# Cross-attention and mixture-of-experts kernel: scores head by head, rounds in three steps, and value products of 33 columns

## The chip, the cores and the metric

The kernel runs on one core of a Trainium2 chip. The metric is the device time of one launch in microseconds (us); lower is better. Times are given as the median of several runs, and one execution was recorded by the hardware profiler.

## What is computed

Inputs are x and ctx, both 8 x 512 x 256 in fp32. For each of the 8 batch rows an mLSTM-like attention with 8 heads of 32 columns runs over 512 positions, with q from x and k = v = ctx; then a feed-forward layer with 2 shared and 8 routed experts (top 2) follows.

```
ifg = concat(q, k, v);  ig = ifg @ igate_w.T + b;  log_f = log_sigmoid(ifg @ fgate_w.T + b)
log_D = cumsum(log_f)[s] - cumsum(log_f)[t] + ig[t]      (t <= s, else -inf)
D = exp(log_D - max(log_D))
C = (q_h @ k_h.T / sqrt(32)) * D                         (per head h)
h = C @ v_h / (max(|sum C|, exp(-max log_D)) + 1e-6)
x = x + layernorm(h) * ln_scale
u = layernorm(x);  x = x + u + shared_experts(u) + top2 routed_experts(u)
```

## The kernel before

The program is two blocks. The second runs the routed experts (39 tiles of 256 sorted tokens) and is not changed. The first, some 760 us of the span, does the attention, the router and the shared experts batch by batch. Only the attention's rounds in it are changed.

**The attention of a batch** is cut into J = 4 chunks of P = 128 positions. Positions of earlier chunks reach a later one through a state matrix (`state`, line 1022), so each chunk j is one round that works on a diagonal block of 128 x 128 positions for all NH = 8 heads. A round has these parts:

- exponents, on TensorE (lines 1037 and 1039): for each half of four heads (g = 0, 1) a bf16 product of the identity with the causal mask (128 rows, 512 columns) starts a bank and a bf16 product of `exp_lhs` with `exp_rhs` (56 rows, 512 columns) adds the exponents. Banks 0 and 1 of the four attention banks.
- decay, on ScalarE (line 567): exp of both banks into `decay`.
- scores, on TensorE (line 1048): for each g one fp32 product of k (`qcT`) with `qmask`, 128 rows and 512 columns, into banks 2 and 3. `qmask` holds q four times, each copy zeroed outside the 32 rows of one head. Half of it is made by VectorE (line 698, four multiplications of 128 x 512), half by GpSimd (line 475, four too).
- ct, on VectorE (line 767): scale, scores and decay multiplied, two operations of 128 x 512.
- value products, on TensorE: the state's part (line 1066, for j > 0, bank 0), and then for each head a product of ct with `vaug` (line 1071). A head's values are 33 columns (32 and a column of ones for the row sum), but each product streams PW = 99 columns, of which 33 are used.
- hn, on VectorE (lines 775, 781 and 783): the results out of PSUM, two operations per round for the values and one more for the state's part.

**The order** of the first block is written out by hand: `START`, `FIRST`, `ORDER` and `ORDER_6` are lists of letters, and every engine walks them and does its own part of each letter. "U" is one unit of the shared experts (16 per batch): up products (line 1119), gelu and a rounding on ScalarE (lines 590 and 593), a subtraction on VectorE (line 835), and, two units later, down products (line 1102). The digits are the steps of the rounds: each digit is written twice, the first for exponents and scores of a round, the second for its value products. They run in pass b for batch b + 1, between the units of batch b. "S" is the state, "L" the last down products of the batch before, "H" the handing over of the tokens to the shared experts (lines 629 and 849), "Y" the finished sum (line 842) and its store. "A", "Q", "B", "D", "E" belong to the router; "F", "G", "M", "R", "C", "c" to the front of the batch after (norm, transposes, gates, cumulative sums); "T", "V", "W", "X" to the norms after the attention. Batch 0's attention stands in `START`, where no units run yet; "w" there is the splitting of one piece of the shared weights (ScalarE line 622 or 624, VectorE line 678 or 681).

```
ORDER = "S 0 L H Y 0 U 1 A U 1 F U Q 2 U F 2 B U P 3 U 3 D U G M T E U T U Z T U Z R V U V U V U R U W U X C U c".split()
```

## Time and profile before

| what | value |
|---|---|
| median of 3 runs | 1243.25 us (1241.1 to 1245.12) |
| the profiled execution | 1241.27 us |
| its span | 1239.5 us |
| TensorE busy | 1137.4 us |
| VectorE busy | 919.4 us |
| ScalarE busy | 837.6 us |
| GpSimd busy | 341.8 us |
| TensorE's mean granted clock | 0.964 |

A profile row names an instruction by its source line, engine, operation and tiles. The timeline gives start (us), duration (us) of a merged group, and in brackets how long the engine had been idle before it and what ended the idle time. Matmuls are pipelined: the durations of neighbours overlap, so the pitch is read from start to start. One fp32 product on TensorE appears as two matmul records (a group "x4" is two products); a transpose and an fp32r or bf16 product appear as one.

### The profile page before, as it was taken

The numbers are of one execution on the slowest core, as the hardware profiler recorded it, in microseconds if no ns is written. First come the engines' busy times: TensorE is split into PE (matmuls) and PEld (weight loads), VectorE is DVE, ScalarE is ACT, GpSimd is POOL, SyncE is SP. The second block draws the span as 40 slices with busy tenths as digits, with TensorE's granted clock in tenths as the row PEclk, the third lists the DMA queues.
The fourth block names the chain that finished last, engine by engine and source line by source line (L and its number), as shares of the span: only waits on it lengthen the run. The fifth ranks groups of instructions, "written<-read, shape, count | busy, mean of one in ns | idle before, by whom it ended". The sixth has DMA issues, their size and how long they took to land. (4 is left out here: it accounts for less than half of the span.)

```text
span 1239.5 us, 21821 instructions
## 1 busy us (share of the span) xinstructions
PE 1137.4 (92%) x7861; PEld 996.7 (80%) x7861; DVE 919.4 (74%) x2215; ACT 837.6 (68%) x1441; POOL 341.8 (28%) x319
## 2 busy tenths in 40 slices
PE   2748999999989999989989897999999999999996
PEld 1436776886777777777868787999999999999996
DVE  5885696686777777866955564888888888888883
ACT  3526556566476556565664353999999999999994
POOL 7121221510510412313113020233333233333333
PEclk9776999999999999999999898999999999999998
DMA  6110011111010100110001035788888888888872
GB/s 197 34 35 17 34 36 35 36 35 35 35 52 23 65 27 32 46 35 35 19 17 44 1 121 170 219 220 233 239 212 232 244 208 232 244 209 230 246 186 27
DMA packets 141692, 136.17 MB, mean 110 GB/s; under 512 B 48599, under 2 KB 127585, under 8 KB 141585
## 3 DMA queue, kind: packets, MB, share of 16 engines
q1 hardware_dynamic: 122948, 111.68, 28.6%
q0 software_dynamic: 14304, 18.75, 9.2%
q10 hardware_dynamic: 4332, 4.34, 1.0%
q8 instruction: 63, 1.03, 0.3%
q14 instruction: 45, 0.36, 0.1%
HBM read 109.42 MB, written 25.33 MB: 109 GB/s over the span
## 5 line engine op out<-in xcount | busy, mean ns | idle before, releaser
L1358 DVE TENSOR_TENSOR wlo<-big,whi 128x512 fp32r<-128x512 f32 x312 | 219.9, 716 | 21.8 <-ACT whi L1311 14.4
L1311 ACT CAST whi<-big 128x512 fp32r<-128x512 f32 x312 | 191.2, 615 | 6.5 <-PEq L420 5.1
L590 ACT ACTIVATE shared_hraw<-bank,b1s 128x512 f32<-128x512 f32 x128 | 88.1, 688 | 153.9 <-PE bank L1119 153.6
L1283 PE MATMUL bank<-xhi,whi 128*128 128x256 f32 x624 | 175.6, 281 | 6.3 <-DVE xlo L1372 5.1
L1261 PE MATMUL bank<-whi,hhi 128*128 128x256 f32 x624 | 178.1, 285 | 0.0
L1283 PE MATMUL bank<-xhi,wlo 128*128 128x256 f32 x624 | 174.5, 280 | 0.0
L1261 PE MATMUL bank<-wlo,hhi 128*128 128x256 f32 x624 | 174.4, 280 | 0.0
L1261 PE MATMUL bank<-whi,hlo 128*128 128x256 f32 x624 | 174.4, 280 | 0.0
L1283 PE MATMUL bank<-xlo,whi 128*128 128x256 f32 x624 | 174.3, 279 | 0.0
L1333 ACT ACTIVATE hraw<-bank,b 128x256 f32<-128x256 f32 x312 | 147.9, 474 | 36.2 <-PE bank L1283 35.3
L835 DVE TENSOR_TENSOR shared_hlo<-shared_hraw,shared_hhi 128x512 fp32r<-128x512 f32 x128 | 93.1, 731 | 96.4 <-ACT shared_hhi L593 92.9
L495 POOL DMA_INDIRECT sorted_tokens<-rowbuf,slots x64 | 66.7, 1042 | 322.5 <-DVEq L911 305.5
L1102 PE MATMUL bank<-whs,shared_hhi 128*128 128x256 f32 x512 | 150.2, 293 | 3.8 <-DVE shared_hlo L835 3.8
L1402 DVE TENSOR_TENSOR hlo<-hraw,hhi 128x512 fp32r<-128x512 f32 x156 | 108.0, 693 | 55.3 <-ACT hhi L1338 49.7
L1102 PE MATMUL bank<-whs,shared_hlo 128*128 128x256 f32 x512 | 146.0, 285 | 0.0
L1102 PE MATMUL bank<-wls,shared_hhi 128*128 128x256 f32 x512 | 145.9, 285 | 0.0
L1436 POOL DMA_INDIRECT out_dram<-yt,token x78 | 135.4, 1736 | 29.3 <-issue 18.7
L1119 PE MATMUL bank<-xhs,whs 128*128 128x512 f32 x256 | 118.1, 461 | 9.5 <-ACT shared_hraw L590 5.9
L1283 PEld LDWEIGHTS bank<-xhi,whi 128*128 128x128 f32 x624 | 118.9, 190 | 6.7 <-POOL xhi L1425 5.3
L1283 PEld LDWEIGHTS bank<-xlo,whi 128*128 128x128 f32 x624 | 119.0, 191 | 0.0
L1283 PEld LDWEIGHTS bank<-xhi,wlo 128*128 128x128 f32 x624 | 118.2, 189 | 0.0
L1261 PEld LDWEIGHTS bank<-whi,hhi 128*128 128x128 f32 x624 | 117.7, 189 | 0.0
(275 smaller groups left out, 2634.6 us busy)
## 6 DMA issues: line engine op xcount, KB each, us to landing
big<-in_L_ffn_W_r_dram SPq DMA_DIRECT2D x78, 1024.0 KB, 7.4
qcT<-sorted_tokens SPq DMA_DIRECT2D x39, 260.0 KB, 2.9
xb<-in_x_dram SPq DMA_DIRECT2D x8, 512.0 KB, 4.6
cb<-in_ctx_dram SPq DMA_DIRECT2D x8, 512.0 KB, 3.5
xr<-in_x_dram SPq DMA_DIRECT2D x8, 512.0 KB, 3.5
out_dram<-base ACTq DMA_DIRECT2D x8, 512.0 KB, 2.9
sorted_tokens<-chunk SPq DMA_DIRECT2D x9, 260.0 KB, 3.4
out_dram<-yt,token POOLq DMA_INDIRECT x78, 4.0
```

Source lines behind the costliest of these rows:

```text
L495: nc.gpsimd.indirect_dma_start(out=xs_dram, out_offset=bass.IndirectOffsetOnAxis(ap=slots[:, k, j:j + 1], axis=0), in_=rowbuf[:, j, :], in ...
L590: nc.scalar.activation(hraw[:, k % NHB, :], up_bank[k % 2][:, :], ACT.Gelu, bias=b1s[:, k // M, k % M:k % M + 1]).then_inc(gelu_done, 1)
L835: tt(hlo[:, k % NHB, :], hraw[:, k % NHB, :], hhi[:, k % NHB, :].bitcast(fp32), ALU.subtract).then_inc(hlo_ready, 1)
L1102: last = mm(down_bank[j // 2][:, (j % 2) * D:(j % 2 + 1) * D], h[:, k % NHB, j * P:(j + 1) * P], w[:, e, wsl], start=k == 0 and t == 0 and ...
L1119: last = mm(up_bank[k % 2][:, :], w[:, e, wsl], x_[:, c, :], start=c == 0 and t == 0, stop=c == KD - 1 and t == 2)
L1261: last = nc.tensor.matmul(y_bank[i][j * D // 512][:, (j * D) % 512:(j * D) % 512 + D], l[:, h, j * P:(j + 1) * P], w[i][:, wsl], start=m = ...
L1283: last = nc.tensor.matmul(ub[:, 0:T], w[i][:, wsl], x_[i][:, k, :], start=k == 0 and t == 0, stop=k == KD - 1 and t == 2)
L1311: nc.scalar.copy(whi[i][:, psl], raw[i][:, psl]).then_inc(t_whi, 1)
L1333: nc.scalar.activation(hraw[:, m % NHB, :], psum[m % NU][:, 0:T], ACT.Gelu, bias=b1[i][:, m:m + 1]).then_inc(t_gelu, 1)
L1358: nc.vector.tensor_tensor(wlo[i][:, psl], raw[i][:, psl], whi[i][:, psl].bitcast(fp32), ALU.subtract).then_inc(t_wlo, 1)
L1402: nc.vector.tensor_tensor(hlo[:, h - 1:h + 1, :], hraw[:, h - 1:h + 1, :], hhi[:, h - 1:h + 1, :].bitcast(fp32), ALU.subtract).then_inc(t_ ...
L1436: nc.gpsimd.indirect_dma_start(out=out_r, out_offset=bass.IndirectOffsetOnAxis(ap=token[n % NG][:, j:j + 1], axis=0), in_=yt[i][:, j, :], ...
```

## The change

The scores are taken head by head. `qmask` and its eight multiplications per batch are gone, with the head mask. Each round now has eight fp32 products of 32 rows and 128 columns: head g * 4 + r reads its own 32 rows of k and q, and the four heads r = 0 to 3 write to four different banks. Since exponents use banks 0 and 1, the scores now have to wait for the decay. ct is four operations of 256 elements, one per r. The value products stream PW = 33 columns per head, all into bank 3, and the state's part goes to bank 2, so hn takes one operation of 264 elements. The exponents are issued as two mask products and then two exponent products. A round takes three steps of the order: exponents (ScalarE's decay in the same step), scores (with ct), value products (with hn). The units are laid between them anew.

```
-    PW = 3 * VW
+    PW = VW
...
-        ORDER = "S 0 L H Y 0 U 1 A U 1 F U Q 2 U F 2 B U P 3 U 3 D U G M T E U T U Z T U Z R V U V U V U R U W U X C U c".split()
+        ORDER = "S H 0 L 0 Y U 0 1 U 1 A U 1 2 F U 2 Q U 2 3 F U 3 P U 3 B U D G M T E U T U Z T U Z R V U V V U R U W U X C U c".split()
...
-                    for r in range(HG):
-                        last = nc.gpsimd.tensor_scalar(qmask[:, 1, r, :], qcT[:, 1, :], headmask[:, r:r + 1], None,
-                                                       ALU.mult)
-                    last.then_inc(qmask_pool, 1)
...
-                    for r in range(HG):
-                        last = ts(qmask[:, 0, r, :], qcT[:, 0, :], headmask[:, r:r + 1], None, ALU.mult)
-                    last.then_inc(qmask_dve, 1)
...
                     for j in range(J):
+                        yield
                         dve.wait_ge(score_done, J * b + j + 1)
                         dve.wait_ge(decay_ready, J * b + j + 1)
-                        for g in range(KD):
-                            last = stt(ct[:, g * HG:(g + 1) * HG, :],
-                                       banks(b, j)[2 + g][:, :].rearrange("p (h s) -> p h s", s=P), SCALE,
-                                       decay[:, g * HG:(g + 1) * HG, :], ALU.mult, ALU.mult)
+                        for r in range(HG):
+                            last = stt(ct[:, :, :].rearrange("p (g r) s -> p g r s", r=HG)[:, :, r, :],
+                                       banks(b, j)[r][:, 0:KD * P].rearrange("p (g s) -> p g s", s=P), SCALE,
+                                       decay[:, :, :].rearrange("p (g r) s -> p g r s", r=HG)[:, :, r, :], ALU.mult, ALU.mult)
...
-                        for g in range(KD):
-                            pvv = banks(b, j)[2 + g][:, 0:HG * PW].rearrange("p (h e) -> p h e", e=PW)[:, :, 0:VW]
-                            dst = hn[:, j, g * HG:(g + 1) * HG, :]
-                            if j > 0:
-                                last = tt(dst, dst, pvv, ALU.add)
-                            else:
-                                last = nc.vector.tensor_copy(dst, pvv)
-                        last.then_inc(hn_ready, 1)
+                            tt(hn[:, j, :, :], hn[:, j, :, :], pvv, ALU.add).then_inc(hn_ready, 1)
+                        else:
+                            nc.vector.tensor_copy(hn[:, j, :, :], pvv).then_inc(hn_ready, 1)
...
+                    def exponents(j):
                         cj = slice(j * P, (j + 1) * P)
-                        if b > 0 and j > 0:
-                            pe.wait_ge(hn_ready, J * b + j)
                         if b == 0 and j > 1:
                             pe.wait_ge(hn_ready, j - 1)
-                        if j == 3 and b > 0:
-                            pe.wait_ge(counts_read, b)
-
                         for g in range(KD):
                             mm(banks(b, j)[g][:, :], identb[:, :], causal[:, :].unsqueeze(1).to_broadcast([P, HG, P]),
                                start=True, stop=False)
+                        for g in range(KD):
                             last = mm(banks(b, j)[g][:, :], exp_lhs[:, cj],
                                       exp_rhs[:, j, g * HG:(g + 1) * HG, :].rearrange("p h s -> p (h s)"),
                                       start=False, stop=True)
                         last.then_inc(exp_done, 1)
+
+                    def scores(j):
+                        cj = slice(j * P, (j + 1) * P)
+                        pe.wait_ge(decay_ready, J * b + j + 1)
                         if j == 0:
                             pe.wait_ge(state_ready, b + 1)
-                            pe.wait_ge(qmask_dve, b + 1)
-                            pe.wait_ge(qmask_pool, b + 1)
+                        elif b > 0:
+                            pe.wait_ge(hn_ready, J * b + j)
                         for g in range(KD):
-                            last = mm(banks(b, j)[2 + g][:, :], qcT[:, KD + g, cj], qmask[:, g, :, cj], start=True, stop=True)
+                            for r in range(HG):
+                                last = mm(banks(b, j)[r][:, g * P:(g + 1) * P], qcT[r * DH:(r + 1) * DH, KD + g, cj],
+                                          qcT[r * DH:(r + 1) * DH, g, cj], start=True, stop=True)
                         last.then_inc(score_done, 1)
...
-                                mm(banks(b, j)[0][:, g * HW:(g + 1) * HW], qcT[:, g, cj], state[:, g, j - 1, :],
+                                mm(banks(b, j)[2][:, g * HW:(g + 1) * HW], qcT[:, g, cj], state[:, g, j - 1, :],
...
-                            last = mm(banks(b, j)[2 + h // HG][:, (h % HG) * PW:(h % HG + 1) * PW], ct[:, h, :],
+                            last = mm(banks(b, j)[3][:, h * VW:h * VW + PW], ct[:, h, :],
```

`START`, `FIRST` and `ORDER_6` are rewritten in the same way. In `ORDER` eight units now stand between S and D where six stood, and eight behind D where ten stood.

How the order moves, at three places. First TensorE in batch 0, one round as it is issued (mask, exponents, scores, the state's part, values; the exponents are those of the round ahead), before and then after:

```order
L1037 MATMUL bank<-causal,identb 128x512
L1039 MATMUL bank<-big,exp_lhs 128x512
L1037 MATMUL bank<-causal,identb 128x512
L1039 MATMUL bank<-big,exp_lhs 128x512
L1048 MATMUL bank<-big,qcT 128x512 x2
L1066 MATMUL bank<-state,qcT 128x132 x2
L1071 MATMUL bank<-vaug,chunk 128x99 x8
```

```order
L1016 MATMUL bank<-causal,identb 128x512 x2
L1019 MATMUL bank<-big,exp_lhs 128x512 x2
L1033 MATMUL bank<-qcT 128x128 x8
L1054 MATMUL bank<-state,qcT 128x132 x2
L1058 MATMUL bank<-vaug,chunk 128x33 x8
```

The two kinds of exponent products no longer alternate, the two scores products have become eight, and the value products stay eight and are narrower.

Second, ScalarE where a round's first decay stands in `ORDER` (the last rows of `exp_rhs`, then the decay of round 0, "H" and "Y"), before and after:

```order
L555 ACTIVATE big<-big,negsel 24x4x128 x4
L567 ACT_TABLE_LOAD
L567 ACTIVATE chunk<-bank 128x512 x2
L629 CAST xhs<-unT 128x1024
L597 DMA out_dram<-base 128x4x256
L590 ACT_TABLE_LOAD
```

```order
L544 ACTIVATE big<-big,negsel 24x4x128 x4
L619 CAST xhs<-unT 128x1024
L556 ACT_TABLE_LOAD
L556 ACTIVATE chunk<-bank 128x512 x2
L587 DMA out_dram<-base 128x4x256
L580 ACT_TABLE_LOAD
```

The cast of the tokens, 128 x 1024, has moved ahead of the first decay.

Third, ScalarE from the decay of round 1 to the router's exp (`prob`), before and after:

```order
L567 ACT_TABLE_LOAD
L567 ACTIVATE chunk<-bank 128x512 x2
L601 ACTIVATE prob<-logits 128x32
L590 ACT_TABLE_LOAD
L590 ACTIVATE shared_hraw<-bank,b1s 128x512
```

```order
L556 ACT_TABLE_LOAD
L556 ACTIVATE chunk<-bank 128x512 x2
L580 ACT_TABLE_LOAD
L580 ACTIVATE shared_hraw<-bank,b1s 128x512
L583 CAST shared_hhi<-shared_hraw 128x512
L591 ACT_TABLE_LOAD
L591 ACTIVATE prob<-logits 128x32
L580 ACT_TABLE_LOAD
```

The router's exp no longer stands beside a decay, so it brings a pair of table loads of its own.

## Rows read from the trace of the kernel before

**Rows 1.** The page's busy times and shares of the span, by engine.

```profile
PE 1137.4 (92%) x7861; PEld 996.7 (80%) x7861; DVE 919.4 (74%) x2215; ACT 837.6 (68%) x1441; POOL 341.8 (28%) x319
```

**Rows 2.** Busy time in one stretch of 40 us: PE, PEld, DVE, ACT, POOL, clock, DMA, GB/s.

```profile
400.00:440.00 40.00, 39.20 (x233) 31.95 (x234) 30.34 (x82) 22.77 (x33) 15.84 (x13) 1.00 0.16 54
```

**Rows 3.** TensorE's waits from 120 to 765 us: total, times, longest.

```profile
PE bank L1037 <- ACT big L555: 11.9, 6, 2.3
...
PE bank L1071 <- DVE chunk L767: 4.0, 6, 0.7
```

**Rows 4.** TensorE's timeline, rounds 0 and 1 of one batch, up to round 2.

```profile
368.49 0.38 PE L1037 MATMUL bank<-causal,identb 128*128 128x512 bf16 x1 [2.30 <-ACT big L555]
...
376.24 0.40 PE L1119 MATMUL bank<-xhs,wls 128*128 128x512 f32 x1
376.48 0.39 PE L1037 MATMUL bank<-causal,identb 128*128 128x512 bf16 x1
376.81 0.39 PE L1039 MATMUL bank<-big,exp_lhs 56*128 56x512 bf16 x1
...
377.76 1.98 PE L1048 MATMUL bank<-big,qcT 128*128 128x512 f32 x4
...
379.82 0.39 PE L1119 MATMUL bank<-xls,whs 128*128 128x512 f32 x1
...
382.31 2.03 PE L1071 MATMUL bank<-vaug,chunk 128*128 128x99 f32 x16 [0.68 <-DVE chunk L767]
...
387.02 0.39 PE L1037 MATMUL bank<-causal,identb 128*128 128x512 bf16 x1
```

**Rows 5.** TensorE's timeline, the same batch: value products of round 3, front, logits, next batch.

```profile
404.53 0.61 PE L1066 MATMUL bank<-state,qcT 128*128 128x132 f32 x4
404.98 1.92 PE L1071 MATMUL bank<-vaug,chunk 128*128 128x99 f32 x16
406.74 0.60 PE L1146 MATMUL bank<-ident,gate 128*8 128x128 f32 x4
...
410.03 0.38 PE L990 MATMUL bank<-ident,qn 128*128 128x128 f32 x2
...
442.24 1.85 PE L1088 MATMUL bank<-cent,unT 128*128 128x8 f32 x16
443.94 0.45 PE L1007 MATMUL bank<-ident,rows 72*128 72x72 f32 x4
...
454.73 0.38 PE L1037 MATMUL bank<-causal,identb 128*128 128x512 bf16 x1 [2.29 <-ACT big L555]
```

**Rows 6.** ScalarE's timeline, the opening of the same batch.

```profile
370.84 1.05 ACT L629 CAST xhs<-unT 128x1024 fp32r<-128x1024 f32 x1
...
375.84 1.28 ACT L590 ACT_TABLE_LOAD   x1 [3.95 <-DVE base L842]
377.13 0.69 ACT L590 ACTIVATE shared_hraw<-bank,b1s 128x512 f32<-128x512 f32 x1
...
378.49 1.28 ACT L567 ACT_TABLE_LOAD   x1
379.78 1.08 ACT L567 ACTIVATE chunk<-bank 128x512 f32<-128x512 f32 x2
```

**Rows 7.** VectorE's timeline, the same batch: ct, finish, mask, last unit.

```profile
371.78 1.29 DVE L767 SCALAR_TENSOR_TENSOR chunk<-bank,chunk 128x512 f32<-128x512 f32 x2 [3.92 <-PE bank L1048]
...
374.12 1.28 DVE L842 TENSOR_TENSOR base<-base,bank 128x512 f32<-128x512 f32 x2
...
412.75 2.90 DVE L698 TENSOR_SCALAR big<-qcT,headmask 128x512 f32<-128x512 f32 x4 [1.90 <-ACT qcT L529]
...
449.16 1.12 DVE L835 TENSOR_TENSOR shared_hlo<-shared_hraw,shared_hhi 128x512 fp32r<-128x512 f32 x1 [1.68 <-ACT shared_hhi L593]
```

**Rows 8.** VectorE and ScalarE in batch 0: gates and the cumulative sum.

```profile
25.88 0.63 ACT L540 ACTIVATE frow<-frow 24x512 f32<-24x512 f32 x1
...
27.61 0.68 DVE L707 TENSOR_TENSOR frow<-frow 24x512 f32<-24x512 f32 x1
```

More of the change, by code:

```diff
@@ L116, in xattn_moe_kernel @@
         take_two = A("take_two", [KE, 1])
-        headmask = A("headmask", [P, HG])
+        A("space", [P, HG])
         blockmask = A("blockmask", [P, HG, VW])
@@ L144, in xattn_moe_kernel @@
         qn = A("qn", [P, J, D])
-        qmask = big[0][:, :].rearrange("p (g r s) -> p g r s", g=KD, r=HG)
         norm_x, norm_u = ((A(f"bn6_{n}", [P, J, 6]), A(f"mv_{n}", [P, J, 2]), A(f"nw_{n}", [P, 5, J])) for n in "xu")
@@ L282, in _ @@
                                         base=0, pattern=[[1, NE], [-1, NE]], channel_multiplier=0)
-                nc.gpsimd.affine_select(out=headmask[:, :], in_=headmask[:, :], compare_op=ALU.is_ge, fill=0.0,
-                                        base=0, pattern=[[-DH, HG]], channel_multiplier=1)
                 nc.gpsimd.affine_select(out=blockmask[:, :, :], in_=blockmask[:, :, :], compare_op=ALU.is_ge,
@@ L295, in _ @@
                     pool.wait_ge(s_const, 2 + r)
-                nc.gpsimd.affine_select(out=headmask[:, :], in_=headmask[:, :], compare_op=ALU.is_ge, fill=0.0,
-                                        base=DH - 1, pattern=[[DH, HG]], channel_multiplier=-1)
                 nc.gpsimd.affine_select(out=blockmask[:, :, :], in_=blockmask[:, :, :], compare_op=ALU.is_ge,
@@ L348, in xattn_moe_kernel @@
         NW = (J - 1) * (J - 1) * NH
-        START = "f f f f w w w f f w w f f S w w w 0 w w 0 w w 1 w w g 1 w 2 w g 2 3 3 g T T T V V g g V W h g u g u X g".split()
-        FIRST = "S 0 U 0 1 A U 1 F U Q 2 U F 2 B U P 3 U 3 D G M T E U T U T R V U V U V U R U W U X C U c".split()
-        ORDER = "S 0 L H Y 0 U 1 A U 1 F U Q 2 U F 2 B U P 3 U 3 D U G M T E U T U Z T U Z R V U V U V U R U W U X C U c".split()
-        ORDER_6 = "S 0 L H Y 0 U 1 A U 1 U Q 2 U 2 B U P 3 U 3 D U T E U T T U V U V V U W U X U U U U".split()
+        START = "f f f f w w w f f w w f f S w w w 0 w w 0 0 w w 1 w w 1 g 1 w 2 2 w g 2 3 3 3 g T T T V V g g V W h g u g u X g".split()
+        FIRST = "S 0 U 0 U 0 1 A U 1 U 1 2 F U 2 Q U 2 3 F U 3 P U 3 B U D G M T E T U T R V U V U V R U W X C U c".split()
+        ORDER = "S H 0 L 0 Y U 0 1 U 1 A U 1 2 F U 2 Q U 2 3 F U 3 P U 3 B U D G M T E U T U Z T U Z R V U V V U R U W U X C U c".split()
+        ORDER_6 = "S H 0 L 0 Y U 0 1 U 1 A U 1 2 U 2 Q U 2 3 U 3 P U 3 B U D T E U T T U V V V U W U X U U U U".split()
         assert ORDER.count("U") == U and ORDER_6.count("U") == U and FIRST.count("U") + START.count("u") == U and START.count("w") == PIECES
@@ L772, in back @@
                         dve.wait_ge(pv_done, J * b + j + 1)
+                        pvv = banks(b, j)[3][:, 0:NH * VW].rearrange("p (h e) -> p h e", e=VW)
                         if j > 0:
                             rr = eexp[:, NW + (j - 1) * NH:NW + j * NH].unsqueeze(2).to_broadcast([P, NH, VW])
-                            own.done(tt(hn[:, j, :, :], banks(b, j)[0][:, 0:NH * VW].rearrange("p (h e) -> p h e", e=VW),
+                            own.done(tt(hn[:, j, :, :], banks(b, j)[2][:, 0:NH * VW].rearrange("p (h e) -> p h e", e=VW),
                                         rr, ALU.mult))
-                        for g in range(KD):
-                            pvv = banks(b, j)[2 + g][:, 0:HG * PW].rearrange("p (h e) -> p h e", e=PW)[:, :, 0:VW]
-                            dst = hn[:, j, g * HG:(g + 1) * HG, :]
-                            if j > 0:
-                                last = tt(dst, dst, pvv, ALU.add)
-                            else:
-                                last = nc.vector.tensor_copy(dst, pvv)
-                        last.then_inc(hn_ready, 1)
+                            tt(hn[:, j, :, :], hn[:, j, :, :], pvv, ALU.add).then_inc(hn_ready, 1)
+                        else:
+                            nc.vector.tensor_copy(hn[:, j, :, :], pvv).then_inc(hn_ready, 1)
                         yield
@@ L1026, in back @@
                     yield
-                    def scores(j):
+                    def exponents(j):
                         cj = slice(j * P, (j + 1) * P)
-                        if b > 0 and j > 0:
-                            pe.wait_ge(hn_ready, J * b + j)
                         if b == 0 and j > 1:
                             pe.wait_ge(hn_ready, j - 1)
-                        if j == 3 and b > 0:
-                            pe.wait_ge(counts_read, b)
                         for g in range(KD):
@@ L1052, in back @@
-                    pe.wait_ge(exp_act, b + 1)
-                    if b == 0:
-                        pe.wait_ge(s_const, 6)
-                        scores(0)
-                    for j in range(J):
-                        if b > 0:
-                            scores(j)
-                        elif j + 1 < J:
-                            scores(j + 1)
+                    for j in range(J):
+                        if j == 0:
+                            pe.wait_ge(lhs_ready, b + 1)
+                            pe.wait_ge(exp_act, b + 1)
+                            if b == 0:
+                                pe.wait_ge(s_const, 6)
+                        if b > 0 or j == 0:
+                            exponents(j)
+                        yield
+                        if b == 0 and j + 1 < J:
+                            exponents(j + 1)
+                        scores(j)
```

7 lines of the change are left out of this document (2 added, 5 removed).

## The prediction

> **What bounds the kernel now.** I read the page's busy times first. TensorE is busy 92% of the span, VectorE 74%, ScalarE 68%, GpSimd 28% [rows 1]. The change touches only the attention in the first block, so the busy times of a stretch there come next: in the 40 us from 400 on TensorE is busy 39.20, VectorE 30.34, ScalarE 22.77, at full granted clock [rows 2]. So work taken off TensorE shortens this block, as long as the engines that feed it keep up. TensorE's waits show where they don't: 11.9 us in all at the opening of a batch's rounds, for ScalarE's last rows of exp_rhs, and 4.0 us for ct, up to 0.7 a batch [rows 3]. The timeline of one opening shows both: 2.30 us before the exponents and 0.68 us before the value products of round 1 [rows 4]. In ScalarE's timeline [rows 6] the reader should see that its opening is a chain without room: it waits 3.95 us for the finished sum, then loads a table, does gelu and cast of unit 0, loads the exp table, and does the decay of round 1, which ends at 380.86, 12.4 us after the exponents of round 0 began. That chain matters more than its 68%.
>
> **TensorE's work per round.** Each term is a pitch, start to start.
>
> Exponents now: four products that alternate between two row heights, at 0.33 us each (376.48 to 376.81), while neighbours of one height follow each other in 0.24 us (376.24 to 376.48) [rows 4]. So a change of row height costs some 0.09 us. From the first exponents to the scores it is 369.76 - 368.49 by the same pitch, 1.28 us. Grouped two by two, two of the four changes fall away: 2 x 0.24 + 2 x 0.33, about 1.1 us. I take 0.18 us less.
>
> Scores now: they start at 377.76, and the second product behind them starts at 379.82, a pitch of 0.24 after its neighbour [rows 4]. They hold TensorE for 379.82 - 0.24 - 377.76 = 1.82 us, for 2 products of 512 columns. After: 8 products of 128 columns, which is the same number of columns, in 16 matmul records instead of 4. No row shows 32-row products in four different row groups and banks, so I bound them. From above: nothing overlaps. An fp32 record with a weight load of its own costs 0.110 us at 99 columns (16 in 406.74 - 404.98 = 1.76 us) and 0.106 us at 8 columns (16 in 443.94 - 442.24 = 1.70 us) [rows 5]; 16 records are 1.76 us. From below: four row groups run at once, a quarter of that, 0.44 us. Between them lies what I take: products start in order, and the two records of one product need the same rows, so each waits for its twin but the next head's first record can run beside the twin. Then a product costs one record's time, 8 x 0.107 = 0.86 us. To each value come two changes of row height, 0.2 us. I take 1.06 us in place of 1.82, with 0.64 and 1.96 as ends.
>
> The Trainium skill, page "TensorE: Matmul & The Clock Gate", section "Part 3: Packing small matmuls", reports four 32-row tiles of 512 columns running 3.07 times as fast as one after another. By it the scores would take 1.82 / 3.07 = 0.6 us, near my lower end; its tiles are four times as wide and one product each, which is why I don't take it.
>
> Value products: 33 columns for 99. Between 99 and 8 columns a record loses only 0.004 us [rows 5], so the width is not what they cost; the weight load, one for each record, is. I take 0.05 us less per round, where two thirds of the columns go.
>
> A round on TensorE is then 0.18 + 0.76 + 0.05 = 0.99 us shorter. If all of it were gained, 4 rounds in 7 batches that run under units would give 27.7 us.
>
> **What the opening of a batch gives back.** The scores now wait for the decay, and "H" stands ahead of it. I count from the start of exponents 0 (368.49). ScalarE ends its exp_rhs at about -0.1, then casts the tokens (1.05), loads the exp table (1.28) and does the decay (1.08) [rows 6]: 3.3. TensorE has done exponents (1.1) and the last down products (1.45, half a unit; a unit is 2.85 us, since 387.02 - 382.31 - 1.76 = 2.95 with its entry [rows 4]) by 2.6, so it waits 0.8. Scores to 4.5. VectorE's ct comes as four operations in place of two that took 1.29 us together [rows 7]; an estimate of 1.6 with the fixed part twice. It ends at 6.1, the finished sum (1.28) [rows 7] at 7.4. ScalarE: issue of the store 0.4 (375.84 less 374.12 + 1.28 [rows 6, 7]), table 1.28, gelu and cast 378.49 - 377.13 = 1.36, table 1.28, decay of round 1 1.08 [rows 6]: 12.8, where it ended at 12.4 before. TensorE has long done value products 0, exponents 1 and unit 1 (some 10.4), so it waits over 2 us for this decay, where before the scores of round 1 needed no decay. Scores to 13.9, unit 2 to 16.7, state's part (404.98 - 404.53 = 0.45 [rows 5]) and values (1.71) to 18.9. Exponents 2 began at 387.02 - 368.49 = 18.5 before, with the same three units done [rows 4]. So rounds 0 and 1 gain nothing and lose 0.4 us.
>
> Rounds 2 and 3 have a whole unit (2.85 us) between exponents and scores, against a decay of 1.08 us and a table load of 1.28, so nothing stands in their way. The router's exp now brings a pair of table loads of its own, 2 x 1.28 us on ScalarE. They fall under unit 2 and the values of round 1, 5 us in which ScalarE has only a gelu to do. Rounds 2 and 3 gain 2 x 0.99 = 2.0. Per batch: 2.0 - 0.4 = 1.6 us, and 7 batches 11.2 us.
>
> **Behind the rounds.** VectorE no longer makes its half of qmask, 2.90 us in one piece while the chain of the norms waits behind it [rows 7]; GpSimd, busy 28% [rows 1], gets time back that nobody on the path waits for. One unit of cover (2.85 us) moves from this stretch into the rounds (8 units where 9 stood from the front's transposes on, the first before them included), so TensorE reaches each wait 2.85 us earlier and VectorE's chain is 2.90 us and one unit's subtraction shorter: they keep step, and I cost both at nothing. If they did not, un and rows would be late next. The 2.30 us wait before the exponents stays: VectorE's part of exp_rhs stands behind the last unit's subtraction, which waits 1.68 us for ScalarE [rows 7], and that piece of order is not changed. ct costs VectorE 0.3 us more a round and hn some 0.1 less.
>
> **Batch 0 has no units.** VectorE's mask goes, but ScalarE's last gate operation ends at 25.88 + 0.63 = 26.51, and VectorE's sum began at 27.61 [rows 8], so 1.1 us is gained. In the rounds exponents of the next round now stand in front of the scores and wait for hn, which costs about what the shorter products save. Zero for them.
>
> **Sum.** 11.2 + 1.1 = 12.3 us off. The profiled execution took 1241.27 us, with a span of 1239.5, so 1229.0 by it; the median of the runs is 2 us above it at 1243.25, and from the median it is 1231.0. I predict the median: 1231.0 us. A difference of 0.3%, 3.7 us, is about what a measurement of this kernel can tell from none.
>
> **The rivals.**
> 1. Four row groups overlap fully. Scores cost 0.64 instead of 1.06 us; 0.42 x 4 rounds x 7 batches is 12 us more: 1219 us. For it: four heads in a row write four banks. Against: the twin records.
> 2. Nothing overlaps, because weight loads go one after another: the slower side. The value products show that a record costs its weight load, 0.106 us even at 8 columns [rows 5], and 16 loads are four times as many as before. Scores cost 1.96 us, 0.9 more than I take, on the chain in all four rounds: 25 us, so 1256 us, slower. It decides from the point where the scores cost over 1.55 us. The same page of the Trainium skill, section "Part 2", says that a weight load of 32 rows takes as long as one of 128, for it is the columns that count; no row here shows a 32-row load of 128 columns by itself.
> 3. Each change of row group costs what a change of row height does, 0.09 us: 8 in a round, 0.7 x 4 x 7 = 20 us on top of rival 2, 1276 us. The row for it is the pitch of 0.33 against 0.24 [rows 4]. The page "TensorEngine Tiling (Array Packing)" of the Trainium skill, section "Key Properties", says that a change of tiling mode drains the engine but that tiles of one mode are independent; by that only the two changes I count cost something.
> 4. The waits eat it: ScalarE's chain is late in rounds 2 and 3 too, or the norms' chain is. 1.6 us a batch are enough: 1242 us, no change.
>
> **Chances.** My forecast 0.38, rival 1 0.22, rival 2 0.24, rival 3 0.06, rival 4 0.10. Rivals 1 and the forecast are faster by over 0.3%; with 0.02 of rival 4 that is 0.62. Within 0.3%: most of rival 4 and cases between the forecast and rival 2, 0.12. Slower: 0.26. The range reaches from 1212 (rival 1, with the opening losing 1 us a batch less than I count) to 1257 (rival 2); it leaves out rival 3 and the tails. For the faster cases alone it would be 1212 to 1237.
>
> **What would show it.** A scores group of a round should hold TensorE for about 1.1 us (0.6: rival 1; 2.0: rival 2; over 2.5: rival 3). Exponents: 1.1 us. Value products: still some 1.7 us. In TensorE's waits a new one on the decay should stand, about 0.8 and 2 us in rounds 0 and 1, 3 us a batch, and none in rounds 2 and 3. The wait for exp_rhs should stay at about 2.3 us. From one batch's first exponents to the next it takes 454.73 - 368.49 = 86.2 us now [rows 4, 5] and should take 84.6. Wrong it is if that period falls by over 3 us, or not at all.

## The result, and the profile after

The changed kernel is slower: 1259.32 us (median of 4 runs, 1257.74 to 1261.56) against 1243.05 us (4 runs, 1241.1 to 1245.12) for the kernel before, a ratio of 1.0132 with an interval of 1.0107 to 1.0157. The forecast was 1231.0 with a range of 1212 to 1257.

That ratio has to be read with care. Beside the experiments, measured later, the kernel before took 1255 to 1258 us and the changed one still 1259 to 1261, so that the ratio there was 1.0043 and 1.0033. All three intervals lie above 1, but how large the loss is hangs on the measurement of the kernel before. So I compare every experiment with the kernel before as it was measured beside it, and with `after_again` or `after_third`, the changed kernel itself once more.

The profiled execution of the changed kernel took 1257.74 us, its span is 1256.0, TensorE's mean granted clock 0.935. Against [rows 1] TensorE has 10.0 us less to do, VectorE 23.7 and GpSimd 54.5 less, ScalarE 16.5 more; the span is 16.5 us longer all the same.

```profile
PE 1127.4 (90%) x8245; PEld 1007.6 (80%) x8245; DVE 895.7 (71%) x2215; ACT 854.1 (68%) x1453; POOL 287.3 (23%) x284
```

**Where the 16.5 us are.** ScalarE's last rows of exp_rhs (line 555 before, 544 after) open the rounds of a batch, so they cut the span into comparable pieces. Before, then after: the first opening, the second, the last, and TensorE's first product of the second block.

```profile
38.71 2.56 ACT L555 ACTIVATE big<-big,negsel 24x512 bf16<-24x512 bf16 x4
107.65 2.56 ACT L555 ACTIVATE big<-big,negsel 24x512 bf16<-24x512 bf16 x4
...
625.94 2.56 ACT L555 ACTIVATE big<-big,negsel 24x512 bf16<-24x512 bf16 x4
...
765.43 0.30 PE L1245 MATMUL bank<-ident,qcT 128*128 128x128 f32 x1 [2.20 <-PEq L420]
```

```profile
36.94 2.56 ACT L544 ACTIVATE big<-big,negsel 24x512 bf16<-24x512 bf16 x4 [0.15 <-DVEq L729]
113.69 2.56 ACT L544 ACTIVATE big<-big,negsel 24x512 bf16<-24x512 bf16 x4
...
636.26 2.56 ACT L544 ACTIVATE big<-big,negsel 24x512 bf16<-24x512 bf16 x4
...
778.59 0.30 PE L1232 MATMUL bank<-ident,qcT 128*128 128x128 f32 x1 [2.20 <-PEq L413]
```

| piece | before | after | difference | before_again to after_again |
|---|---|---|---|---|
| to the first opening | 38.71 | 36.94 | -1.8 | -2.7 |
| batch 0 (first to second opening) | 68.94 | 76.75 | +7.8 | +7.0 |
| six batches (second to last opening) | 518.29 | 522.57 | +4.3 | -6.5 |
| last opening to the second block | 139.49 | 142.33 | +2.8 | +3.0 |
| second block | 474.07 | 477.41 | +3.3 | +3.6 |

The last column has the same differences between two later profiles, of the same two kernels measured side by side (the second series below); they add up to 4.4 us. Batch 0 and the end of the block lose in both columns. The six batches between lose 4.3 us in one and gain 6.5 in the other, because there the kernel before takes 532.1 us for them in place of 518.3. The second block is not changed; over all profiled executions it takes 474.1 to 479.7 us, and what moves it stays open.

**TensorE's waits** from 120 to 780 us in the trace of after (total, times, longest):

```profile
PE bank L1033 <- ACT chunk L556: 14.9, 10, 2.2
PE bank L1016 <- ACT big L544: 9.7, 6, 2.3
PE bank L1067 <- DVE rowbuf L800: 9.3, 1, 9.3
PE bank L991 <- DVE rows L701: 7.1, 6, 1.3
...
PE bank L974 <- ACT frow L596: 4.5, 6, 0.8
```

The wait for exp_rhs stays (11.9 in [rows 3]) and the one for ct is off the list's head (4.0 there). New are the scores' wait for the decay, which comes as 2.15 us in round 1 of each of six batches and as 0.5 us in round 0 of four of them, and two waits in the front of the batch after: rows, and frow, which had 0.8 us in all before. At the end of the block 9.3 us stand in one piece, for the norms of the last batch; the same wait in the trace of before:

```profile
PE bank L1080 <- DVE rowbuf L816: 3.1, 1, 3.1
```

**One opening**, TensorE's timeline of after, and what it waits for up to the next opening. It answers to [rows 4] and [rows 5].

```profile
376.13 0.59 PE L1016 MATMUL bank<-causal,identb 128*128 128x512 bf16 x2 [2.29 <-ACT big L544]
...
377.19 0.58 PE L1089 MATMUL bank<-whs,shared_hhi 128*128 128x256 f32 x1
...
380.04 0.97 PE L1033 MATMUL bank<-qcT 32*128 32x128 f32 x16
...
384.37 0.60 PE L1016 MATMUL bank<-causal,identb 128*128 128x512 bf16 x2
384.89 0.60 PE L1019 MATMUL bank<-big,exp_lhs 56*128 56x512 bf16 x2
385.43 0.50 PE L1106 MATMUL bank<-xhs,whs 128*128 128x512 f32 x1
...
389.23 0.73 PE L1033 MATMUL bank<-qcT 32*128 32x128 f32 x16 [2.15 <-ACT chunk L556]
389.88 0.50 PE L1106 MATMUL bank<-xhs,whs 128*128 128x512 f32 x1
...
394.78 1.87 PE L1058 MATMUL bank<-vaug,chunk 128*128 128x33 f32 x16
396.49 0.60 PE L1016 MATMUL bank<-causal,identb 128*128 128x512 bf16 x2
...
420.60 0.41 PE L974 MATMUL bank<-ident,qn 128*128 128x128 f32 x2 [0.76 <-ACT frow L596]
...
453.12 0.74 PE L991 MATMUL bank<-ident,rows 72*128 72x72 f32 x4 [1.21 <-DVE rows L701]
...
464.46 0.59 PE L1016 MATMUL bank<-causal,identb 128*128 128x512 bf16 x2 [0.78 <-ACT big L544]
```

Start to start, the scores hold TensorE for 389.88 - 389.23 = 0.65 us (1.82 before), the exponents 385.43 - 384.37 = 1.06 (1.28 before), the values 1.71 (1.76 before). That is 1.4 us off each round. But the scores of round 1 stand 2.15 us in wait for the decay, and the last down products, which the prediction has at 1.45 us, take 380.04 - 377.19 = 2.85 us: some 1.1 us behind the 2.29 us wait TensorE falls to its lower level, 1.2 GHz. Three microseconds of the same down products before and after, the granted clock third from the end:

```profile
369.00:372.00 3.00, 3.00 (x11) 1.48 (x11) 0.22 (x1) 2.67 (x4) 0.00 (x0) 1.00 0.07 24
```

```profile
378.00:381.00 3.00, 3.00 (x27) 2.65 (x26) 0.18 (x1) 1.30 (x3) 0.00 (x0) 0.57 0.00 0
```

A wait of that length alone doesn't bring the clock down: the kernel before has waited 2.30 us here too and keeps 1.00.

The period splits in two, by the first exponents of rounds 0 and 2 and of the next batch. From round 0 to round 2 it was 18.53 us [rows 4] and is 20.36. Over the six openings from the third on, before takes 18.5 us in four (clock 1.00) and 19.8 to 19.9 in two (0.91); after takes 19.1 in one (1.00), 19.4 in three (0.91) and 20.4 in two (0.83). The means are 19.0 and 19.7. From round 2 to the next batch it was 67.71 [rows 4, 5] and is 67.97, though two rounds in it are 1.4 us shorter each.

**The stretches**: busy time of PE, PEld, DVE, ACT and POOL, clock, DMA, GB/s. Batch 0's rounds, then one period of a later batch; first before, then after.

```profile
44.00:94.00 50.00, 29.89 (x140) 18.89 (x139) 41.98 (x122) 17.49 (x28) 7.32 (x5) 0.84 0.13 43
280.00:366.00 86.00, 82.63 (x502) 65.71 (x501) 63.76 (x177) 52.33 (x73) 20.53 (x19) 1.00 0.11 38
```

```profile
44.00:100.00 56.00, 36.79 (x181) 26.66 (x180) 36.43 (x117) 16.15 (x27) 1.04 (x1) 0.58 0.10 34
286.00:373.00 87.00, 78.89 (x545) 64.81 (x544) 60.57 (x177) 54.85 (x75) 13.63 (x15) 0.98 0.11 37
```

In the later batch TensorE's busy time falls by 3.7 us (the 5.6 of four rounds, less some 2, which I put down to the lower clock), but its idle time rises from 3.4 to 8.1. In batch 0 the clock falls from 0.84 to 0.58.

### The profile page after: what moved, and what is told of

It reads as the page before. It is cut to its first block and busy times, and to the rows that moved or that the text cites. A ratio compares the mean times of both kernels' runs of the same rounds, so it can differ in the third digit from the quotient of the medians.

```text
span 1256.0 us, 22586 instructions
## 1 busy us (share of the span) xinstructions
PE 1127.4 (90%) x8245; PEld 1007.6 (80%) x8245; DVE 895.7 (71%) x2215; ACT 854.1 (68%) x1453; POOL 287.3 (23%) x284
## 5 line engine op out<-in xcount | busy, mean ns | idle before, releaser
L1089 PE MATMUL bank<-wls,shared_hhi 128*128 128x256 f32 x512 | 149.3, 292 | 0.0
L1089 PE MATMUL bank<-whs,shared_hlo 128*128 128x256 f32 x512 | 149.2, 291 | 0.0
L1423 POOL DMA_INDIRECT out_dram<-yt,token x78 | 135.7, 1740 | 29.2 <-issue 18.5
L1106 PE MATMUL bank<-xhs,whs 128*128 128x512 f32 x256 | 114.8, 448 | 8.4 <-ACT shared_hraw L580 4.8
```

The source lines that it names most:

```text
L1089: last = mm(down_bank[j // 2][:, (j % 2) * D:(j % 2 + 1) * D], h[:, k % NHB, j * P:(j + 1) * P], w[:, e, wsl], start=k == 0 and t == 0 and ...
L1106: last = mm(up_bank[k % 2][:, :], w[:, e, wsl], x_[:, c, :], start=c == 0 and t == 0, stop=c == KD - 1 and t == 2)
L1423: nc.gpsimd.indirect_dma_start(out=out_r, out_offset=bass.IndirectOffsetOnAxis(ap=token[n % NG][:, j:j + 1], axis=0), in_=yt[i][:, j, :], ...
```

## The experiments

My theory after the result had three parts: **(a)** batch 0 lost to the clock, **(b)** the openings lost to a decay that comes late, **(c)** the end of the block lost to the unit that moved away. Rivals: the shorter score products themselves, the narrower value products (less activity, lower clock), or the bare wait for the decay.

### First series: which part of the change is it? (kernel before: 1257.93 us)

**narrow_before** and **wide_after**, the width alone: `PW = VW` in the kernel before, `PW = 3 * VW` in the changed one.

> The kernel before with only PW = VW: 33 columns per value product instead of 99, everything else as before. Theory 1 (the loss comes from new waits in which TensorE's clock falls, 0.935 granted in the changed kernel against 0.964): no wait is new here, so the time is 1241 to 1244 us and the clock stays at about 0.964; a record still costs some 0.107 us. Theory 3 (the narrower and 32-row products themselves lower the granted clock): slower, 1247 us or more, and a clock below 0.955.

> The changed kernel with only PW = 3 * VW: its value products stream 99 columns again, in the new banks. Theory 1 (new waits, clock): 1258 to 1262 us, clock near 0.935. Theory 3 (narrow products lower the clock): faster than the changed kernel by 4 us or more, clock above 0.945. Theory 2 (the order's cover alone): no difference, 1259 to 1261 us.

Measured: narrow_before 1264.3 us, 1.0036 (1.0013 to 1.0059); wide_after 1257.5, 0.9997 (0.9979 to 1.0016). The narrow products alone gain nothing: 0.36% slower. The granted clock of narrow_before is 0.954 in its profile, where Theory 1 said 0.964, and its batch 0 takes 72.7 us (69.0 in before_again) at a clock of 0.76 from 44 to 94 us, where the kernel before has 0.84. So part of Theory 3 holds in the kernel before: fewer columns, a lower clock, more time. In the changed kernel the width brings back nothing: batch 0 of wide_after takes 77.6 us.

**whole_scores**: the changed kernel with the old score products.

```
-                            for r in range(HG):
-                                last = mm(banks(b, j)[r][:, g * P:(g + 1) * P], qcT[r * DH:(r + 1) * DH, KD + g, cj],
-                                          qcT[r * DH:(r + 1) * DH, g, cj], start=True, stop=True)
+                            last = mm(banks(b, j)[2 + g][:, :], qcT[:, KD + g, cj], qmask[:, g, :, cj], start=True, stop=True)
```

`qmask`, its multiplications on VectorE and GpSimd and the two operations of ct come back with it; the three-step order and the wait for the decay stay.

> The changed kernel with the old scores: two 128-row products of 512 columns per round from qmask into banks 2 and 3, ct in two operations, in the new order of three steps and with the wait for the decay. Scores take 1.82 us instead of 0.66 on TensorE, and qmask costs VectorE 2.9 us a batch again. Theory 2 (the order is at fault, the shape of the scores is a pure gain): 4 x 1.16 us x 7 batches more, up to 1290 us, and not below 1275. Theory 1 (part of the gain of the scores is lost to the clock, which falls less when TensorE has more to do): granted clock above 0.95 and 1265 to 1278 us. Theory 3 (32-row products lower the clock): clock 0.96 and at most 1262 us.

Measured: 1299.09 us, 1.0293 (1.0246 to 1.034). That is 9 us above what Theory 2 allowed. In the new order the head-by-head scores, with the work on `qmask` that they save, are worth some 40 us (41.6 beside wide_after in the same series). The score products themselves are 4 x 1.17 x 7 = 33 of it; the rest I put down to `qmask`. So the shorter products are not what costs, and the loss is to be looked for around them. The head-by-head scores in the old order of two steps were not run.

**filled**: idle products (bf16, 512 columns, into a bank that the next step overwrites) stand in front of the two waits of the opening, to keep TensorE's clock up.

```
+                        for _ in range(9 if b > 0 and j == 1 else 4 if b > 0 and j == 0 else 0):
+                            mm(banks(b, j)[3][:, :], identb[:, :], causal[:, :].unsqueeze(1).to_broadcast([P, HG, P]),
+                               start=True, stop=True)
                         pe.wait_ge(decay_ready, J * b + j + 1)
```

Nine more stand before the wait for exp_rhs.

> The changed kernel with idle products (identity times mask, 512 columns, results overwritten) on TensorE: nine before the wait for the exponents of round 0 and four and nine before the waits for the decays of rounds 0 and 1, in batches 1 to 7. Theory 1 (waits let the clock fall): the clock rises to 0.95 or more, and the time falls to 1254 us or less; the stretch from the first exponents of a batch to the next gets shorter by 1 us or more. Theory 2 (cover): nothing gained, 1258 to 1264 us.

Measured: 1267.02 us, 1.0063 (1.0041 to 1.0085), clock 0.942. A miss of both theories: the mean clock goes from 0.935 to 0.942, and the time goes up by some 8 us. The idle products are themselves late. ScalarE's last rows of exp_rhs, the nine idle products and the exponents behind them:

```profile
380.82 2.56 ACT L544 ACTIVATE big<-big,negsel 24x512 bf16<-24x512 bf16 x4
382.98 2.11 PE L1044 MATMUL bank<-causal,identb 128*128 128x512 bf16 x9
384.92 0.59 PE L1016 MATMUL bank<-causal,identb 128*128 128x512 bf16 x2
```

The rows are there at 383.38 and the exponents start 1.5 us later, where after has 0.14; it is so in four of the six batches, and in round 1 of each the idle products end 0.8 us behind the decay. That makes some 10 us, about what is lost. So whether a higher clock in the openings would gain time is not settled by this run.

### Second series: the end and the opening (kernel before: 1255.54 us)

**after_again** and **before_again** are the two kernels unchanged.

> The changed kernel once more, since the kernel before took 1258 us on the chip of the first four runs and 1243 us elsewhere. Theory 1 and 2: 1257 to 1261 us wherever it runs, the clock near 0.935; whether the kernel before is 1243 or 1258 us beside it says whether the chip matters to that one alone.

> The kernel before, for a profile from this chip. If it takes 1243 us, its trace has no waits put down to a remote releaser. If it takes 1258 us, ScalarE and VectorE should show the waits put down to a remote releaser that the narrow variant of it showed, 2 to 5 us once a batch after the last round.

Measured: after_again 1260.66 us, 1.0043 (1.0028 to 1.0058); before_again 1256.22, 1.0004 (0.999 to 1.0018). So the changed kernel repeats, and the kernel before is what differs from the first measurement. One place where it does, ScalarE's timeline of before_again:

```profile
413.14 0.62 ACT L593 CAST shared_hhi<-shared_hraw 128x512 fp32r<-128x512 f32 x1
418.89 0.57 ACT L606 COPY frow<-bank 8x512 f32<-8x512 f32 x1 [5.13 <-remote]
```

and the same instructions in the first profile:

```profile
404.02 0.62 ACT L593 CAST shared_hhi<-shared_hraw 128x512 fp32r<-128x512 f32 x1
407.38 0.58 ACT L606 COPY frow<-bank 8x512 f32<-8x512 f32 x1 [2.74 <-PE bank L1146]
```

The router's copy starts 2.4 us later behind its neighbour, and the profile names no engine that it waited for. Waits of that kind are fewer than expected (two of this size in eight batches), but a usual period of before_again is 87.6 us in place of 86.3. What holds it stays open.

**cover6**: in the last pass one unit moves back ahead of the last "V", as cover for the norms.

```
-... P U 3 B U D T E U T T U V V V U W U X U U U U
+... P U 3 B U D T E U T T U V U V V U W U X U U U
```

> The changed kernel with one unit of the last pass moved: ORDER_6 has two more places of cover between the V steps and one unit less behind X. Theory 2 (in the last pass the norms' chain on VectorE has lost its cover, TensorE waits 9.3 us for rowbuf there against 3.1 us before): 3 to 6 us faster than the changed kernel beside it, the wait for rowbuf down to 4 to 7 us. If the end is not bound by that wait: no difference.

Measured: 1256.75 us, 1.0019 (1.0001 to 1.0036), 3.9 us below after_again, though the two intervals overlap a little. The wait it aims at is a third of what it was, and another has grown by 2.5 us from the 2.2 of after_again, in its list of TensorE's waits:

```profile
PE bank L1089 <- DVE shared_hlo L819: 4.7, 2, 2.5
...
PE bank L1067 <- DVE rowbuf L800: 3.1, 1, 3.1
```

From the last opening to the second block it takes 138.5 us where after_again takes 142.5 and before_again 139.5. So (c) holds by the traces: some 6 us of wait gone, 4.0 of time, the rest given back.

**opening**: the last down products stand between exponents and "H", and "A" moves one unit up.

```
-        ORDER = "S H 0 L 0 Y U 0 1 U 1 A U 1 2 F ..."
+        ORDER = "S 0 L H 0 Y U 0 1 A U 1 U 1 2 F ..."
```

> The changed kernel with the opening of ORDER as S 0 L H 0 Y U 0 1 A U 1 U 1 2: the token cast behind the first decay again and the router's exp beside the decay of round 1. Theory 1 (the wait of TensorE for the decay, 2.2 us in round 1, costs its length and the clock after it): the decay of round 0 comes 1 us earlier, 0.5 to 1.5 us a batch less, 3 to 8 us faster in all, and the clock a little up. If the chain behind the finished sum sets the opening: no difference, within 2 us.

Measured: 1260.6 us, 1.0044 (1.003 to 1.0058): no difference from after_again. "H" is not what makes the decay of round 1 late: TensorE's wait for it is still 2.1 us.

### Third series: the finished sum, batch 0 (kernel before: 1256.7 us)

ScalarE's timeline of after shows what does:

```profile
378.23 1.08 ACT L556 ACTIVATE chunk<-bank 128x512 f32<-128x512 f32 x2
...
384.14 1.28 ACT L580 ACT_TABLE_LOAD   x1 [4.82 <-DVE base L826]
...
388.09 1.09 ACT L556 ACTIVATE chunk<-bank 128x512 f32<-128x512 f32 x2
```

Between the two decays ScalarE stands 4.82 us for VectorE's finished sum ("Y"); it was 3.95 before [rows 6], when no scores needed the decay. The sum stands in VectorE's order behind ct of round 0, which since the change waits for the scores, which wait for the decay. The sum itself needs only the last down products.

**early_finish**: "Y" moves ahead of the scores of round 0, in `ORDER` and `ORDER_6`.

```
-        ORDER = "S H 0 L 0 Y U 0 1 U 1 ..."
+        ORDER = "S H 0 L Y 0 U 0 1 U 1 ..."
```

> The changed kernel with Y (finished sum and store of the batch before) moved ahead of the second step 0 in ORDER and ORDER_6: S H 0 L Y 0 U 0 1. If the wait of TensorE for the decay of round 1 (2.2 us, behind the finished sum on ScalarE) costs its length: it falls under 0.5 us, the period of a batch from 87.4 to 85.5 us, 10 to 14 us faster than the changed kernel. If that time is taken up again by later waits (the rows, the last unit): wait gone, period 87 us, under 3 us faster.

Measured: 1251.57 us, 0.9958 (0.9936 to 0.998). The wait for the decay all but goes, from 14.9 us, in early_finish's list:

```profile
PE bank L991 <- DVE rows L701: 7.2, 6, 1.2
...
PE bank L1033 <- ACT chunk L556: 1.5, 3, 0.5
```

8 to 9 us gained for one letter beside after_third and after_again, a little under the forecast, so (b) holds. From the exponents of round 0 to those of round 2 it now takes 16.6 to 17.9 us. The row above the wait tells what stays: the front's wait for rows is untouched. Whether the kernel before would gain by the same letter was not tried.

**whole_nowait**: whole_scores without its wait for the decay, which its score banks 2 and 3 don't need.

```
-                        pe.wait_ge(decay_ready, J * b + j + 1)
```

> The kernel with whole scores in the new order (1299 us) without the wait of the scores for the decay: banks 2 and 3 are free of the exponents there. If the decay's wait in the three steps is what the order costs: 12 to 20 us faster than with it, 1280 to 1287 us, and TensorE no longer waits for the decay. If the loss is in VectorE's late subtractions and in the clock: 1293 to 1300 us.

Measured: 1302.27 us, 1.037 (1.0341 to 1.0398): no faster than whole_scores. Its worst wait is another:

```profile
PE bank L1102 <- DVE shared_hlo L833: 17.5, 10, 6.4
```

VectorE, with its half of `qmask` back, is late with a unit's subtraction. The rival of the bare wait falls for that kernel: there the wait only covered another. It says nothing on the changed kernel, whose banks need the wait.

**warm_start**: the changed kernel with idle products in batch 0's rounds alone, ahead of the value products. They compute nothing that is used.

```
+                        if b == 0 and j < J - 1:
+                            for _ in range(8 if j == 0 else 5):
+                                mm(banks(b, j + 1)[3][:, :], identb[:, :], causal[:, :].unsqueeze(1).to_broadcast([P, HG, P]),
+                                   start=True, stop=True)
```

> The changed kernel with idle products in batch 0 alone: eight before the value products of round 0 and five before those of rounds 1 and 2, while TensorE waits for ct. If the clock costs the start (it fell 3.4 us after it had risen in batch 0 and stayed low for 41 us; from the first to the second opening 76 to 77 us against 69 in the kernel before): the clock is granted through batch 0's rounds, that stretch takes 70 to 73 us, 4 to 6 us faster in all. If not: no difference or 1 to 2 us slower.

Measured: 1251.78 us, 0.9969 (0.9948 to 0.9991), some 8 us below the changed kernel. TensorE's timeline of after, the value products of batch 0's rounds 0 and 1:

```profile
47.68 3.63 PE L1058 MATMUL bank<-vaug,chunk 128*128 128x33 f32 x16 [2.66 <-DVE chunk L755]
...
57.57 3.46 PE L1058 MATMUL bank<-vaug,chunk 128*128 128x33 f32 x16
```

and of warm_start:

```profile
47.19 1.97 PE L1062 MATMUL bank<-vaug,chunk 128*128 128x33 f32 x16 [0.83 <-DVE chunk L755]
...
54.10 2.20 PE L1062 MATMUL bank<-vaug,chunk 128*128 128x33 f32 x16
```

The same 16 records take 3.5 us at the lower level and 2 at the upper. From first to second opening batch 0 takes 71.0 us in place of 76.8, near the 68.9 of before: (a) holds. Here TensorE's own products lie on the chain, and in rounds 0 and 1 the idle ones end before ct is there. The gain in batch 0 is 5.8 us; the profiled execution took 1247.86 us, the fastest of all, and the rest of its lead is not batch 0's.

**joined**: early_finish and cover6 together.

> The changed kernel with Y ahead and with the unit moved in ORDER_6. If both gains are real and add up: 1242 to 1250 us, below the kernel before on a chip where that takes 1256. If the opening's wait is taken up again: 1254 to 1257 us.

Measured: 1248.15 us, 0.9933 (0.9908 to 0.9958), 3.4 us below early_finish. They add up, by overlapping intervals again; in the traces the piece from the last opening to the second block goes from 142.7 to 137.3 us.

### Fourth series: all three, and the width again (kernel before: 1255.08 us)

**best** is joined with warm_start's idle products; **best_wide** is best with `PW = 3 * VW`; **after_third** and **wide_third** are the changed kernel and wide_after once more.

> The changed kernel with all three: Y ahead, the unit moved in ORDER_6, idle products in batch 0. If the gains add up (9, 4 and 9 us): 1238 to 1244 us beside 1256 for the kernel before.

> The same with PW = 3 * VW. If narrow value products cost through the clock, as the narrow variant of the kernel before hinted (ratio 1.0036 to before, more time at the low clock): 2 to 6 us faster than with 33 columns, and less time at the low clock. If the width means nothing: within 1.5 us of it.

> The changed kernel as it is, as the reference for the others of this call: 1257 to 1261 us.

> The changed kernel with PW = 3 * VW, beside the changed kernel on one chip, which the first call had not: if the width costs through the clock, 2 to 6 us faster than 33 columns; if not, within 1.5 us.

| kernel | median, us | ratio | interval |
|---|---|---|---|
| best | 1240.97 | 0.9893 | 0.9871 to 0.9914 |
| best_wide | 1231.73 | 0.9825 | 0.9805 to 0.9846 |
| after_third | 1259.22 | 1.0033 | 1.0016 to 1.005 |
| wide_third | 1259.39 | 1.0033 | 1.0018 to 1.0047 |

The three repairs bring 1259.22 - 1240.97 = 18.3 us. The width does nothing in the changed kernel and 9.2 us in best. Both are single pairs of one chip, but of one series, and best and best_wide have intervals that don't touch.

The traces show where the 9.2 us are. In best the last three periods take 87.5 to 88.8 us, in best_wide 84.8; batch 0 takes nearly the same in both (70.3 and 69.9 us), though the clock from 44 to 114 us is 0.66 and 0.78. The stretch from the exponents of round 2 to those of round 3, of the same batch, in best and then in best_wide:

```profile
380.73:393.53 12.80, 12.80 (x78) 10.26 (x78) 8.43 (x32) 7.40 (x9) 0.00 (x0) 0.73 0.00 1
```

```profile
380.74:390.62 9.88, 9.88 (x79) 8.25 (x78) 7.85 (x32) 7.33 (x9) 0.00 (x0) 1.00 0.01 2
```

The profile shows TensorE busy throughout in both, but in best its clock is granted at 0.73. It is so in four batches of best, 3 us each, and in none of best_wide; three batches of early_finish have it too, and none of after. So in best the width pays in one stretch, through the clock. Why the fall comes there, and whether the width or the moment of a fall decides, was not tested by itself and stays open.

best_wide beats both kernels: 1231.73 against 1255.08 and 1259.22 us in one series.

## Why the prediction was wrong

**What held.** The exponents (1.1 us forecast, 1.06 measured) and the values (some 1.7 us, 1.71). The wait for the decay in round 1 ("over 2 us", 2.15) and none in rounds 2 and 3. The wait for exp_rhs (2.3 us, 2.29). The start of batch 0 (1.1 us forecast, 1.8 measured). Of the 0.8 us forecast for round 0 only 0.5 came, and where the clock was low none: TensorE was late itself.

**The scores' term was mis-sized**, to the good side: 1.06 us forecast, 0.65 measured, the 0.64 of rival 1. The twin records do not hold each other up. The Trainium skill's 3.07 ("TensorE: Matmul & The Clock Gate", "Part 3: Packing small matmuls"), by which the prediction had 0.6 us, is borne out here at 1.82 / 0.65 = 2.8 times. So rival 1's premise was right, and its 1219 us failed for other reasons. Rival 2, which ended on the slow side at 1256, gave a time near the measured one by a mechanism that the trace excludes.

**"They keep step, and I cost both at nothing"** is a step that failed. The prediction said what would be late if they did not, un and rows, and so it came: 7.1 us for rows and 4.5 for frow over six batches, and 9.3 us at the last norms where 3.1 stood. From the exponents of round 2 to the next batch the forecast was 2.0 us less; measured are 67.97 us for 67.71. In the last pass there was no mask to save, since VectorE makes its last one (line 698) at 589 us, before the last opening, so nothing could make up for the unit there; cover6 shows what it is worth. For rows and frow it is argued from the list of waits alone, since no run gave that unit back. And against before_again, whose part behind the opening takes 69.1 us, the same part is 1.1 us shorter.

**The opening was priced with the sum in its old place**, a choice and no error of size. The prediction did put ct and the sum in a row on VectorE and found the 2 us wait. It took that for a cost of the change; early_finish shows that it is a cost of one letter, and worth 9 us. From round 0 to round 2 it had 0.4 us more and the traces have 0.7, so as a price of the changed order it was nearly right, though it has no term for the clock, which in two openings of six made 2.85 us of 1.45 of down products.

**"Batch 0 has no units … Zero for them"** failed: +7.8 us. The sum counted instructions at one price each, and the price of the value products doubled (3.46 us for 16 records, where warm_start has 1.97) when the clock went from 0.84 to 0.58. The clock stands in no term of the sum, though the page of before shows it low in just these slices, the second to the fourth of 31 us each, at 7, 7 and 6 tenths:

```profile
PEclk9776999999999999999999898999999999999998
```

warm_start gives most of it back. What brings the clock down is shown in part only: narrower value products alone cost 3.7 us of batch 0 in narrow_before.

Per batch, then: 5.6 us off in place of the prediction's 4.0, and 4.7 more idle and some 2 at the lower clock in place of the 2.4 allowed. Two small slips carry no weight: the scores of round 0 end at 4.4 by the prediction's own terms and not at 4.5, and rival 2 decides from 1.50 us and not from 1.55.

The measured time itself, 2.3 us beyond the range, says less than these steps do. Of the 16.5 us between the first two profiles 3.3 lie in the block that is not changed, and side by side the first block of the changed kernel is 0.8 us longer (780.83 against 780.03 us), where 12.3 less was forecast: batch 0 takes 7.0 us more where none was allowed, and the end 3.0 us more.

## What to carry to other kernels

Making TensorE's products shorter can make the engines that feed them late: after such a change look first at the order of the feeders, and ask of each wait whether the thing waited for could have been issued earlier. Price TensorE's work at the clock that the stretch will have, not the one it had: in batch 0 here less work took more time. Idle products helped where TensorE's own work was on the chain and they ended before the thing waited for was there. Cut both traces into the same pieces, and repeat the kernel before beside the changed one: here the sign of one piece, the six batches, hung on it. And undo the change by parts: here the part that seemed risky was worth some 40 us, and most of the loss lay in three places around it, two of order and one of the clock.

## What the runs showed of the hardware that I had not expected

- Eight fp32 products of 32 rows and 128 columns, in four row groups and four banks, take 0.65 us, 0.041 us for each of 16 records, where a record with 128 rows costs 0.107. The Trainium skill says in Part 2 of "TensorE: Matmul & The Clock Gate" that a load of 32 rows takes as long as one of 128, and the trace of after agrees: a median of 0.187 us against 0.192. But sixteen of them fit in 0.54 us, so loads for different row groups do not go one after another here.
- TensorE's mean granted clock fell from 0.964 to 0.935 in a kernel in which it is still busy 90% of the span. A stretch in which the profile shows no idle time ran at 0.73 in best and at 1.00 in best_wide.
- The same kernel took 1243 and 1256 us in two measurements, the slower with some waits that no engine accounts for, while the changed one repeated within 2 us.
